# Seven block products for the text keys and values, one key stack filled by halves, and probability copies shared with ScalarE, in a cross-attention kernel

## What is computed

```python
ctx_img = context[:, :257]; ctx_txt = context[:, 257:]
q = rms_norm(linear(x, q_w, q_b), norm_q_w)
k = rms_norm(linear(ctx_txt, k_w, k_b), norm_k_w)
v = linear(ctx_txt, v_w, v_b)
k_img = rms_norm(linear(ctx_img, k_img_w, k_img_b), norm_k_img_w)
v_img = linear(ctx_img, v_img_w, v_img_b)
out = linear(attention(q, k, v) + attention(q, k_img, v_img), o_w, o_b)
```

## Time and profile before

| | us |
|---|---|
| median of 3 runs | 1310.32 (1308.32 to 1310.51) |
| the profiled execution, its own time | 1309.53 |
| its span, first to last instruction | 1307.7 |
| busy: PE / DVE / ACT / POOL | 1246.5 / 1003.2 / 709.7 / 396.3 |

### The profile page before, as it was taken

One profiled execution on the slowest core, in us unless ns is written; L12 is line 12 of the kernel. 1 busy time (PEld: TensorE's weight loads), 2 busy tenths in 40 slices (PEclk: granted clock), 3 DMA queues, 4 the chain that ended last, 5 costly groups with the idle time before them and its releaser, 6 DMA issues.

```text
span 1307.7 us, 27645 instructions
## 1 busy us (share of the span) xinstructions
PE 1246.5 (95%) x9016; PEld 991.0 (76%) x9016; DVE 1003.2 (77%) x1749; ACT 709.7 (54%) x1567; POOL 396.3 (30%) x489
## 2 busy tenths in 40 slices
PE   5899999999999999999999999999999869989998
PEld 3677777888888888888888888888888634568886
DVE  3568788877887878788887777887777851479998
ACT  3446555555555555555555555555556511457875
POOL 3533334433344333443334433344332000000000
PEclk9899999999999999999999999999999979989999
DMA  8454557655576555765557655567542896639991
GB/s 273 105 146 118 153 143 193 162 143 148 149 200 168 141 149 149 195 175 138 150 149 190 184 134 151 147 186 190 133 137 65 262 396 238 247 134 364 366 357 47
DMA packets 158884, 237.85 MB, mean 182 GB/s; under 512 B 17792, under 2 KB 95616, under 8 KB 158464
## 3 DMA queue, kind: packets, MB, share of 16 engines
q1 hardware_dynamic: 158848, 237.39, 61.3%
HBM read 142.43 MB, written 17.04 MB: 122 GB/s over the span
## 4 chain that ended last, share of the span: by engine, by line
PE 65%; DVE 11%; issue 9%; SPq 6%; ACT 4%; POOL 3%; DMA 2%; ACTq 0%; DVEq 0%; POOLq 0%
PE ps L900 26%; PE ps L892 10%; PE ps L939 6%; SPq L339 5%; PE ps L1000 5%; DVE small L720 4%; PE ps L1034 3%; PE ps L1114 3%; PE ps L1117 2%; PE ps L1120 2%; ACT kt_hi L559 2%; POOL small L427 2%; DVE small L722 2%; DVE kb L737 2%; PE ps L1135 1%
## 5 line engine op out<-in xcount | busy, mean ns | idle before, releaser
L546 ACT ACTIVATE p<-ps,small 128x512 f32<-128x512 f32 (+2 forms) x400 | 271.8, 679 | 389.7 <-DVE small L722 370.0
L730 DVE COPY pt<-ps 128x512 f32<-128x512 f32 (+1 forms) x400 | 273.2, 683 | 61.9 <-PE ps L892 61.0
L720 DVE TENSOR_REDUCE small<-ps 128x1 f32<-128x512 f32 (+2 forms) x400 | 267.7, 669 | 16.6 <-PE ps L939 16.6
L892 PE MATMUL ps<-ident,p 128*128 128x128 f32 x1584 | 237.5, 272 | 0.8 <-ACT p L546 0.7
L892 PEld LDWEIGHTS ps<-ident,p 128*128 128x128 f32 x1584 | 196.8, 140 | 53.0 <-ACT p L546 1.3
L939 PE MATMUL ps<-k_stack,q_stack 96*128 96x512 f32 (+1 forms) x400 | 192.5, 482 | 26.7 <-ACT p L546 16.5
L722 DVE TENSOR_TENSOR small<-small 128x1 f32<-128x1 f32 x400 | 148.0, 370 | 13.8
L757 DVE TENSOR_TENSOR kt_lo<-ps,kt_hi 128x512 fp32r<-128x512 f32 x99 | 68.5, 692 | 111.2 <-ACT kt_hi L559 111.1
L900 PE MATMUL ps<-w_hi_k,cx_hi 128*128 128x512 f32 x384 | 152.1, 396 | 0.8 <-ACT v_sb L568 0.8
L900 PE MATMUL ps<-w_lo_k,cx_hi 128*128 128x512 f32 x384 | 151.7, 395 | 0.0
L900 PE MATMUL ps<-w_hi_k,cx_lo 128*128 128x512 f32 x384 | 151.5, 395 | 0.0
(11 more groups left out here) (188 smaller groups left out, 1954.8 us busy)
## 6 DMA issues: line engine op xcount, KB each, us to landing
expert<-experts SPq DMA_DIRECT2D x34, 1536.0 KB, 8.9
k_stack<-kt_hi SPq DMA_DIRECT2D x392, 128.0 KB, 2.4
k_stack<-kt_lo SPq DMA_DIRECT2D x196, 128.0 KB, 2.4
cx<-ctx_t SPq DMA_DIRECT2D x24, 1024.0 KB, 5.0
codes<-codes SPq DMA_DIRECT2D x64, 256.0 KB, 3.1
code_scale<-code_scales SPq DMA_DIRECT2D x256, 64.0 KB, 2.6
scaled<-codes SPq DMA_DIRECT2D x64, 256.0 KB, 2.4
weight_q<-scaled SPq DMA_DIRECT2D x1, 4096.0 KB, 13.6
```

Of the source, the lines that this page charges most:

```text
L546: eng.activation(pb[:, lo:hi], ps_s[h % NS][:, lo:hi], exp, bias=nm[1 - par][:, h:h + 1], accum_out=ls[1 - par][:, h:h + 1]).then_inc(e_ex ...
L720: eng.tensor_reduce(ngm[:, h:h + 1], ps_s[h % NS][:, lo:hi], AX.X, ALU.max, negate=True).then_inc(e_gm, 1)
L730: eng.tensor_copy(pt_sb[hp % NPT][:, 0:n], ps_pt[hp % 2][:, 0:n]).then_inc(e_pte, 1)
L892: last = eng.transpose(dst[:, c * P:(c + 1) * P], src[:, c * P:(c + 1) * P], ident[:, :])
```

## The change

1. **Seven products.** The text weights are one matrix of 512 rows and 1024 columns, keys and values side by side. On two tiles of 128 context rows it is a product of 2 x 2 blocks (rows of the two tiles; halves of the 512 inputs; keys and values). Strassen's scheme in Winograd's form makes it from seven block products instead of eight. Each block product is six matmuls of 512 columns (two input chunks by three split products). A pair of tiles takes 42 matmuls, a group 84; it was 96. The numbers of matmuls in the eight slots of a pair are 5, 5, 5, 6, 5, 5, 5, 6.
2. **Sums and splits.** POOL makes four sums of context blocks per pair (128x256) and splits seven blocks, the first two as one (128x512), the other five at 128x256. The sums of the weights are made once, at the start, by POOL (four of 128x1024) and split by ACT and DVE.
3. **Combining.** The seven products share two PSUM banks, taken in turn, and some add onto what is there. Product i+2 of a pair may start only when product i was read: the key bias and first product (L934), then the second product (L941) by DVE; copies of two intermediate sums (`u2_sb`, `p5_sb`) by ACT (L747, at h%8 = 3 and 4); the values as bank plus copy by DVE (L960, at h%8 = 5 and 6, the one of product 4 first); the second key tile by DVE (L948, in slots 0 and 8).
4. **Shift by half a step.** The first pair of group s+1 is made in slots 8 to 15 of step s, the second in slots 0 to 7 of step s+1.
5. **One stack.** There is one key stack. Its heads 0 to 7 are filled behind the last `kt_lo` of the step, its heads 8 to 15 at the start of the next step, 12 transfers each.
6. **Key transposes** move from slots 4, 6, 8, 10 to 5, 7, 9, 10.
7. **Odd probability copies** go to ACT (L728), behind the exp of the slot.
8. **Loop** over six steps instead of two, `code_scale` with one buffer, other places in SBUF for the weights; image part and normalising folded into slots of steps 24 and 26.

```diff
@@ sync, step @@
+                if not loop and s == 0:
+                    eng.wait_ge(e_clo, GT)
+                    load(1, 0)
+                    load(1, 1)
+                if score:
...
+                    stack(1, not loop and s == 1, s * (2 * NPOS) if nxt else None)
...
+                if nxt and (loop or s > 0):
+                    load(s + 1, 1)
+                pass_codes(s, 0, m, loop)
+                if loop or s + 2 < NG:
+                    eng.wait_ge(e_ab, s * (2 * NPOS) + NPOS)
+                    load(s + 2, 0)
+                pass_codes(s, 1, m, loop)
+                if loop or s < NG:
+                    eng.wait_ge(e_klo, s * GT + GT)
+                    if score:
+                        eng.wait_ge(e_qk, s * NH - NH // 2)
+                    stack(0, not loop and s == 0)
@@ scalar, step @@
+                    gp, hp = (g, h - 2) if h >= 2 else (g - 1, h - 2 + NH)
+                    if hp % 2 == 1 and ((score and h >= 2) or (end and h < 2)):
+                        eng.wait_ge(e_pt, gp * NH + hp + 1)
...
+                        eng.activation(pt_sb[hp % NPT][:, 0:n], ps_pt[hp % 2][:, 0:n], copy).then_inc(e_pta, 1)
+                    if norm:
+                        scale_keys(group, j, 1)
...
+                    if cur and h in KT_SLOTS:
...
+                        keys_high(s, KT_SLOTS.index(h), 1)
+                    if (cur if h < NH // 2 else nxt) and h % (NH // 2) in (3, 4):
...
+                        eng.activation(dst[:, :], bank[:, :], copy).then_inc(done, 1)
@@ vector, step @@
+                    if h == 0 and cur:
+                        second_key_tile(-2)
+                    if h == NH // 2 and cur:
+                        second_key_tile(-1)
+                    if cur if p else nxt:
+                        if h % (NH // 2) == 1:
+                            first_key_tile_started(p)
+                        if h % (NH // 2) == 2:
+                            first_key_tile(p)
...
-                    if (score and h >= 2) or (end and h < 2):
+                    if hp % 2 == 0 and ((score and h >= 2) or (end and h < 2)):
...
+                    if cur and h in KT_SLOTS:
+                        keys_low(s, KT_SLOTS.index(h), 1)
+                    if (cur if p else nxt) and h % (NH // 2) in (5, 6):
+                        values(p, 6 - h % (NH // 2))
@@ tensor @@
+                    if i == 0:
+                        eng.wait_ge(e_v, 2 if start else before)
+                    elif i == 1:
+                        eng.wait_ge(e_v if start else e_kb, before)
+                    elif i == 2:
+                        eng.wait_ge(e_kpre, s * 2 + (p + 1))
+                    elif i == 3:
+                        eng.wait_ge(e_kb, before + 1)
+                    elif i == 4:
+                        eng.wait_ge(e_u2, s * 2 + (p + 1))
+                    elif i == 5:
+                        eng.wait_ge(e_p5, s * 2 + (p + 1))
+                    else:
+                        eng.wait_ge(e_v, before + 1)
```

More of the change, by code:

```diff
@@ L20 @@
 IT = 3
+CD = DC // 2
+NPOS = 7
 TXT0 = IMG - 1
@@ L346, in load_matrix @@
+            steps(eng, step)
             def load_matrix(n):
@@ L526, in step, with square_keys, scale_keys @@
-            def step(eng, s, par, loop=False):
-                proj, score, end = parts(s, loop)
-                g = s - 1
-                lo, hi = mask(s, loop)
-                tiles = dict(tiles_of(s, loop)) if proj else {}
+            def square_keys(g, j, n):
+                eng.wait_ge(e_kb, g * GT + j + 1)
+                eng.activation(squares[:, :], kb[KB_OF[j]][:, :], square, scale=D ** -0.5,
+                               accum_out=k_ss[:, j:j + 1]).then_inc(e_sq, n)
+            def scale_keys(g, j, n):
+                eng.wait_ge(e_r, g * GT + j + 1)
+                eng.activation(kb[KB_OF[j]][:, :], kb[KB_OF[j]][:, :], copy, scale=k_r[:, j:j + 1]).then_inc(e_kn, n)
@@ new lines, in step @@
+            def step(eng, s, m, loop=False):
+                cur, nxt, score, end = parts(s, loop)
+                g = s - 1
+                par = m % 2
+                lo, hi = mask(s, loop)
+                if not loop and s == 0:
+                    image()
+                if not loop and s == 1:
+                    eng.wait_ge(e_wlo, NPOS + 1)
+                for h in range(NH // 2 if (not loop and s == 0) else 0, NH):
+                    group, j = {1: (s, 1), 3: (s, 2), 9: (s, 3), 11: (s + 1, 0)}.get(h, (s, None))
+                    norm = j is not None and (nxt if j == 0 else cur)
+                    if norm:
+                        square_keys(group, j, 1)
@@ L705, in step, with image_part @@
-            def step(eng, s, par, loop=False):
-                proj, score, end = parts(s, loop)
+            def image_part(h):
+                if h == 2:
+                    eng.wait_ge(e_orows, 48)
+                    chain(eng.reciprocal(rl, l_st[0]))
+                if h == 4:
+                    chain(eng.tensor_tensor(by_head(o_st[0]), by_head(o_st[0]), rl.unsqueeze(2).broadcast_to((P, NH, HD)), ALU.mult))
+                if h in (6, 8):
+                    chain(eng.tensor_tensor(o_st[0][:, :], o_st[0][:, :], o_rows[:, h // 2 - 2, :], ALU.add))
```

658 lines of the change are left out of this document (416 added, 242 removed).

## The result

The changed kernel takes 1407.67 us (median of 4 runs, 1404.91 to 1409.89), the kernel before 1310.19 beside it: 1.0746 of the time, 95% interval 1.0721 to 1.0771. That is slower, as forecast, but by 97.5 us where 65 were forecast, and 2.7 us above the end of the range. The profiled executions have spans of 1403.2 and 1307.7 us, 95.5 apart.

The account below looks back on a forecast made before the run. It took PE as the old kernel's bound and ACT and DVE chains as the new pace. Terms 50 + 22 + 2 - 1 - 3 - 4 = +66 on 1309.5 gave 1375 us; range 1262 to 1405.

Parts of the forecast that it names:

- Over 22 steps ... +50: Steps 2 to 23: each takes 43.1 us instead of 40.83, adding 50 us in total.
- Step 24 ... -1: Step 24: no products in its second half, but its chain and stack filling stay; 39 instead of 39.9 us, -1.
- the forecast's own case: Steady state: waits on ACT and DVE chains make a step 43.1 us; total 1330 to 1400, chance 0.62.
- a dearer meeting: DVE's running maximum waiting for a POOL instruction: 0.235 us per head, 1.6 a step; at up to 0.34, +68 over 22 steps.
- The five places where the walk had PE wait: PE waits in slots 4, 7, 9, 10 and 12: 0.25, 0.97, 0.95, 1.0 and 1.35 us, together 4.5 a step.
- The stack transfer as releaser of the first scores: Start: the image stack, issued by SP at 65 us behind the third load, releases PE's first scores near 75 us.
- The POOL prices taken between two ends: POOL's 128x256 operations, priced midway between one and 512 columns: 0.74 us for a sum or rest, 0.62 for a high part.
- the first rival: PE stays the bound as DVE and ACT keep up: step 38.1 us, total 1255; chance 0.27 for below 1307.
- Start ... 21.6 later: Before the first scores: POOL's work to 65 us, then load and twelve transfers, 9.9 us; scores at 75.5, +22 in the sum.
- Tail -4, step 25 -3.4: End: image part and a last sum leave the chain, -4 us; every second copy on ACT shortens step 25, -3.4.
- POOL as the bound of the steady state: Rival: 128x256 operations cost nearly their 512 price, POOL needs 46 us a step; +131, total 1440, chance 0.08.
- The one stack: Rival that one stack is too few: decides only if SP's issues exceed 0.647 us, costing at most 1 us a step.

Follow-up runs that it names:

- the kernel with the high part first: Changed kernel with loop written out, row loads first, scalar-operand running maximum, and ACT's high part and sum copy directly behind exp, probability copy last: 1277.40 us.
- the scalar operand: Changed kernel with the running maximum taking the old value as a per-partition scalar instead of a second tensor: 1388.04 us.
- the loads first: Changed kernel with SP issuing step 24's three row loads ahead of the stack's transfers instead of behind them: 1396.79 us.
- the kernel with the stack first: Changed kernel with the image group's key stack issued ahead of the third load instead of behind it: 1406.97 us.
- this copy alone: Changed kernel with ACT's odd-slot probability copy moved behind scaling, high part and sum copy: 1356.38 us.
- the order alone: Changed kernel with only ACT reordered: high part and sum copy directly behind exp, then scaling, output copy, probability copy: 1334.36 us.
- the value-first kernel: Changed kernel with DVE making the value sum of slots 5 and 6 ahead of the key tile's low part: 1412.1 us.

## Where the prediction was right, and the step that failed

**The step that failed** is the sum, in two of its terms. "Over 22 steps ... +50" had nothing for part 8, the loop over six steps, and came to +64.2, of which the two jumps are 9.5. "Step 24 ... -1" had nothing for the loads of the folded image part and came to +12.1. The jumps and step 24 make some 23 of the 30 us between forecast and spans, and they put the time above the range. The range ended at 1405 because its upper end was the forecast's own case with a dearer meeting; a term that was absent had no room in it.

**Right: the sign and the cause.** PE's need fell and the kernel got slower because ACT's and DVE's chains set the step. The five places where the walk had PE wait carry nearly all of its idle time: slot 7 (`v_second`) 19.0 us of the 600, slots 4 and 12 (`u_sb`) 19.0, slot 9 (`kb`) 17.3, slot 10 (`kt_lo`) 9.0. An ordinary step is 43.32 against 43.1 forecast. Most of the rows named as signs came: L971 at 0.373 (over 0.35), first scores near 75 (77.6), POOL with gaps. The stack transfer as releaser of the first scores did not. The POOL prices taken between two ends were 0.738 and 0.628, for 0.74 and 0.62.

**Close by luck in part: 43.1.** It was 37.0 for PE's need and 6.1 of waits (4.5 of the walk, 1.6 of meetings). The waits at the five places are (19.0 + 19.0 + 17.3 + 9.0) / 14 = 4.6 us a step (14 steps in the 600 us), so that PE's own share of 43.3 is 38.7. The waits were 1.5 too long and PE's need 1.7 too small, and the two cancelled. The old kernel's 1.1 us of small waits, which the first rival has in its 38.1, are not in the 43.1. The kernel with the high part first bears out the larger need: its step is 38.62 with almost no named wait left. As for the meetings, the scalar operand put up to 1.2 us on them.

**Other terms and readings.**
- "Over 22 steps": apart from the jumps, the remaining 4.8 us of this term are 0.22 us a step. Of the 9.5 at the jumps, 2.4 came by TensorE's lower clock in the step behind the first, which the prediction did not consider.
- "Step 24": the text named what goes from it and what stays, but not that the folded image part makes DVE wait in slot 2 for loads that SP issues behind twelve stack transfers. What is queued behind that wait on DVE, and ahead of those loads on SP, was not asked. With the loads first the step takes 41.85, still 1.9 more than before, with PE waiting 2.55 us for the stack.
- "Start ... 21.6 later": +23.7, a near hit with the wrong releaser. SP did issue the stack behind the third load, at 67.3 (65 forecast), but in the kernel with the stack first the scores came no earlier; ACT's copy behind POOL's root released PE. The terms as listed add up to 64 us for POOL, not 65, and 65 + 9.9 is 74.9, not 75.5.
- "Tail -4, step 25 -3.4": together -3.8; where the rest went was not looked at.
- The prediction read the two long operations at the start, both stretched, as against the full blocking that the Trainium skill states ("SBUF — State Buffer", Who interferes with whom). The neighbouring rows of the kernel before, DVE and POOL in order of time, show that they agree with it:

```profile
40.09 3.43 DVE L657 TENSOR_TENSOR w_lo_k<-stage_k,w_hi_k 128x2048 fp32r<-128x2048 f32 x1 [0.34 <-ACT w_hi_k L495]
...
40.07 1.30 POOL L457 TENSOR_TENSOR cx_lo<-cx,cx_hi 128x512 fp32r<-128x512 f32 x1
...
44.50 3.21 POOL L457 TENSOR_TENSOR cx_lo<-cx,cx_hi 128x512 fp32r<-128x512 f32 x1
```

If each waits until the other has ended and then takes its undisturbed time (DVE 2.28, POOL 1.04 and 1.29), the four that waited end at 43.65, 44.6, 46.7 and 47.9 us; they end at 43.52, 44.42, 46.57 and 47.71. No sharing is needed to explain the lengths.

**The rivals.** PE bound (1255) did not happen, but the text had the place where it was lost: the copy "lies between exp and high part, for which DVE waits". The experiments put 51 us on this copy alone and 73 on ACT's order; the order alone still left a step of 40.18, and only all five edits together came near PE's bound, at 1277.40. The Trainium skill's advice to move work to Scalar when DVE is saturated ("Perfetto Trace Analysis", Optimizing Scalar/DVE Operations) did not decide by itself here, where DVE was busy 33.8 of 40 us: the same eight copies on ACT lost 0.9 us a step at one place of the slot and gained 1.4 at another. POOL as the bound of the steady state did not come; by the rows it bounds the start. The one stack did not decide the steady state, but at the end of step 24 PE waited 3.07 us for it.

## To carry to other kernels

When work is moved to an engine with slack, the place in its order matters more than its load: put it behind everything that another engine waits for in that slot, and the first operation behind the one that all wait for should be the one with the longest chain behind it. A wait in PE's rows names only where a chain meets PE: with that link taken away part of the wait can come back at the next place, as it did for the value sum, while operations taken out of the chain itself shortened the step by 2.3 us and more. Before a difference of a us or two is read as such a wait, compare the granted clock of the steps. Count the jump of a long loop and every load that a folded-in piece waits for; both are easy to cost at nothing.

## What the runs showed of the hardware

- A jump back over six steps cost PE 4.28 us at the first and 3.40 at the second of two jumps, and POOL 3.62 at the first, of waiting for nothing shown; written out, the place has no gap. The two-step loop before shows no such steps.
- The two-input one-column operation on DVE waits for a running POOL instruction (mean 0.373, up to 1.2 us); with a scalar operand for the second input it takes 0.214, never more than 0.217 in 222 cases, with POOL busy most of the time. The page on the ports in the Trainium skill ("SBUF — State Buffer", Who interferes with whom) names DVE operations with two SBUF inputs, which agrees with this.
- TensorE's granted clock fell from 2.4 to 1.2 GHz at some of PE's pauses: around 420.6 to 427.3 us at the first jump of the change (a pause of 4.28 us), but not at the second (3.40), and in the value-first kernel in 19 of 22 steps, at 577 with a pause of 2.25. At 1.2 GHz the next start behind a score product comes after 0.59 us and behind four transposes after 0.70 (at 422.29 and 425.01), against 0.32 and 0.35 at 2.4 GHz; the step behind the first jump took 45.77 us instead of 43.3.
